# A graph and product-key memory block on one core: the dense head's passes divided 4 and 6 by slot instead of 5 and 5

## The reference, cut to what matters

```python
sim = einsum('pbnhd,pkhd->pbnhk', q, pk_keys)            # two sides, 128 keys each
scores, idx = top_k(sim, 16)                             # best 16 of each side
score = scores[0][..., :, None] + scores[1][..., None, :]
final_scores, pk_idx = top_k(score, 16)                  # best 16 of the pairs
final_scores = softmax(final_scores)
k = einsum('bnhk,bnhkd->bnhd', final_scores, keys_table[ind])    # 16 rows of 16384 per head
v = einsum('bnhk,bnhkd->bnhd', final_scores, values_table[ind])
attn = softmax(causal(einsum('bihd,bjhd->bhij', q_scaled, k)))   # then attn @ v @ Wo
```

## Time and profile before

| what | us |
|---|---|
| runs | 14943.0, 14952.5 (median), 15046.9 |
| profiled execution, its time | 14961.5 |
| its span, first to last instruction | 14959.7 |
| a batch, from its first L571 to the next batch's (14 batches) | 920.0 to 942.5 |

### The profile page before, as it was taken

How to read it: one execution, slowest core, us unless ns; L and a number is a source line. 1 busy time by engine, 2 the same in 40 slices (tenths; PEclk the granted TensorE clock), 3 DMA queues, 4 the chain that set the end, 5 groups by cost and what they waited for, 6 DMA issues and landing times.

```text
span 14959.7 us, 181203 instructions
## 1 busy us (share of the span) xinstructions
PE 8819.9 (59%) x51232; PEld 6784.1 (45%) x51232; DVE 7189.0 (48%) x32006; ACT 4890.6 (33%) x14163; POOL 6799.1 (45%) x7177
## 2 busy tenths in 40 slices
PE   4665655555565565556556555655555555556566
PEld 3444444444444444444444444444444444444454
DVE  5454454544545445444454544445454454544543
ACT  2333333333333333333333333333333333333332
POOL 4444444444444444444444444444444444444444
PEclk7777777777777777777777777777777777777777
DMA  3333333333333333333333333333333333333332
GB/s 93 102 103 103 99 103 101 100 101 100 101 101 104 105 100 102 102 100 103 102 102 100 103 102 100 103 101 104 102 102 104 98 103 104 103 100 96 99 109 92
DMA packets 445985, 1516.88 MB, mean 101 GB/s; under 512 B 123760, under 2 KB 141552, under 8 KB 379248
## 3 DMA queue, kind: packets, MB, share of 16 engines
q0 software_dynamic: 344064, 939.98, 21.3%
q1 hardware_dynamic: 100848, 564.37, 10.9%
HBM read 1499.66 MB, written 4.19 MB: 101 GB/s over the span
## 4 chain that ended last, share of the span: by engine, by line
PE 35%; another core or an unknown queue 27%; DVE 15%; issue 15%; ACT 7%; DVEq 0%; ACTq 0%; DMA 0%; SPq 0%
PE dense_ps L461 13%; PE comb_ps L571 6%; DVE wide L1106 5%; PE wideT_ps L447 5%; ACT expo L697 3%; PE score_ps L498 2%; PE front_ps L401 2%; PE probT_ps L504 2%; PE score_ps L437 2%; DVE onehot L990 1%; DVE onehot L997 1%; DVE hits L1070 1%; ACT wideT L632 1%; ACT prob L737 1%
## 5 line engine op out<-in xcount | busy, mean ns | idle before, releaser
L334 POOL DMA_INDIRECT got<-in_table,rows x7168 | 6797.2, 948 | 8123.9 <-PE comb_ps L571 5913.5
L1106 DVE SCALAR_TENSOR_TENSOR wide<-const_ps,rank,expo 128x128 f32<-128x128 f32 x8192 | 2303.7, 343 | 5572.5 <-remote 4357.0
L461 PE MATMUL dense_ps<-tab,wideT 128*128 128x256 f32 x16384 | 4435.4, 419 | 105.3 <-ACT kv_d L632 53.7
L447 PE MATMUL wideT_ps<-ident,wide 128*128 128x128 f32 x8192 | 1474.6, 311 | 4746.9 <-ACT wideT L632 2784.1
L461 PEld LDWEIGHTS dense_ps<-tab,wideT 128*128 128x128 f32 x16384 | 3338.7, 213 | 845.1 <-issue 309.7
L447 PEld LDWEIGHTS wideT_ps<-ident,wide 128*128 128x128 f32 x8192 | 1134.4, 160 | 5157.4 <-issue 4830.7
L632 ACT ACTIVATE wideT<-wideT_ps 128x512 f32<-128x512 f32 x2048 | 1217.8, 595 | 4674.7 <-remote 3415.3
L697 ACT ACTIVATE expo<-sim_d,shift 128x128 f32<-128x128 f32 x8192 | 2595.1, 393 | 0.6 <-DVEq L1051 0.2
L571 PE MATMUL comb_ps<-got,spread 128*32 128x256 f32 x14336 | 1021.1, 433 | 2.2 <-issue 2.2
L632 ACT ACTIVATE probT<-probT_ps 128x128 f32<-128x128 f32 (+3 forms) x512 | 223.6, 437 | 1556.0 <-remote 1250.7
L571 PEld LDWEIGHTS comb_ps<-got,spread 128*32 128x32 f32 x14336 | 463.8, 123 | 457.1 <-issue 257.5
(11 more groups left out here) (156 smaller groups left out, 8286.8 us busy)
## 6 DMA issues: line engine op xcount, KB each, us to landing
tab<-in_dense SPq DMA_DIRECT2D x512, 1024.0 KB
got<-in_table,rows POOLq DMA_INDIRECT x7168
adj_i<-in_adj SPq DMA_DIRECT2D x16, 1024.0 KB, 7.3
x_in<-in_x SPq DMA_DIRECT2D x16, 256.0 KB
out<-fin SPq DMA_DIRECT2D x16, 256.0 KB, 5.4
tab<-in_wqpk_t SPq DMA_DIRECT2D x1, 512.0 KB, 10.5
tab<-in_keys_t SPq DMA_DIRECT2D x1, 512.0 KB, 15.4
wq_sb<-in_wq SPq DMA_DIRECT2D x1, 512.0 KB, 14.2
```

The lines of the kernel that those rows point to most:

```text
L334: pool.indirect_dma_start(out=got[t % 2][:, g, :], out_offset=None, in_=table, in_offset=bass.IndirectOffsetOnAxis(ap=rows[buf(h)][:, t * ...
L447: mm = pe.transpose(wideT_ps[:, q * P:(q + 1) * P], wide[k % 2][:, q, :], ident[:, :])
L461: mm = pe.matmul(dense_ps[:, v * 2 * D:(v + 1) * 2 * D], wideT[k % 2][:, (2 * u + v) * P:(2 * u + v + 1) * P], tab[(k // CHUNK) % 2][:, (2 ...
L1106: last = dve.scalar_tensor_tensor(wide[k % 2][:, 2 * u + v, :], count_ps[:, v, :], rank1[:, 2 * half + v, key:key + 1], expo[k % 2][:, 2 * ...
```

## The change

The tuples of the middle batches are chosen by slot. The four slots with two passes stay. Every other odd slot (t = 1 or 3) gets `FOUR`, without the pass at w[4], and every other even slot (t = 0 or 2) gets `SIX`, with a second pass at w[0].

```diff
 ONE = (1, 1, 1, 1, 1)
 SIX = (2, 1, 1, 1, 1)
+FOUR = (1, 1, 1, 1, 0)
 FEW = (1, 1, 0, 0, 0)
 NONE = (0, 0, 0, 0, 0)
-MIDDLE = [ONE] + [FEW] * 2 + [ONE] * 12 + [FEW] * 2 + [ONE] * 11
+MIDDLE = [FEW if n in (1, 2, 15, 16) else FOUR if n % 2 else SIX for n in range(SLOTS)]
 ENDING = [SIX] + [FEW] * 2 + [SIX] * 12 + [FEW] * 2 + [SIX] * 2 + [ONE] * 6 + [NONE] * 3
```

## The result

The kernel after takes 15404.3 us (median of 3 runs, 15399.1 to 15409.6), against 14952.5: a ratio of 1.029, interval 1.024 to 1.034. It is slower by 452 us, or 30 us in each of the 15 batches. The forecast was 15095 with a range up to 15310: the sign was right, the size was a third of what came.

What follows compares the result with a forecast made beforehand. The prediction took a gather burst plus serial tail per slot as the bound. Its terms, 19.9 - 20.4 + 13.2 - 3.3 = +9.4 us a batch, +141 us over 15 batches, gave a median of 15095 us, range 14840 to 15310.

Steps and rivals of the forecast that it cites:

- What bounds the kernel: Each slot: about 3 us, a 20 us gather burst stalling TensorE's signals, 3 us more, then a serial tail.
- The sixth pass of the even slots: Second pass at w[0]: +2.96 us per t = 0 slot, +0.35 per t = 2 slot, +19.9 us a batch.
- The fifth pass of the odd slots: Dropping w[4] from the tail starts the move 1.7 us earlier per slot, -20.4 us a batch.
- the give-back: Combining products of ten odd slots after `SIX` fall from 2.26 to 1.93 us, -3.3 us a batch.
- The clock: Odd-slot tails without their multiply partly stay at half clock, slowing later TensorE products: +13.2 us a batch.
- the cold rival: Front and combining products run wholly at half clock: clock term 24 us a batch, 15255 us; chance 0.27.
- What costs nothing: ScalarE and VectorE instructions, SyncE's chunk loads and GpSimd's gather issue were taken to add no time.
- Warm: Rival: shorter tails still bring the clock back, so the clock term goes: 14895 us; chance 0.20.
- Faster: Rival: VectorE's chain slips under the burst, odd tails shorten 2.63 us a slot, clock holds: 14725 us; chance 0.13.

Runs made afterwards that it cites:

- reversed: Kernel before, given four passes (0, 1, 1, 1, 1) in even slots and six in odd ones: 15643.7 us, 1.040, first kind of chip.
- The fill: Kernel after plus four unread products in each four-pass tail: 15215.9 us, 1.011 on the first kind of chip; 9789.0 us, 1.021 on the second.
- slot0_five: Kernel after with five passes in slots 0 and 3: 15291.1 us, 1.024 against the kernel before, first kind of chip.
- the halves: Kernel after with the change kept only in t=0/t=1 slots, or only in t=2/t=3: 9734.8 and 9739.0 us, 1.016 each, second kind of chip.

## Why the prediction was wrong, step by step
**What bounds the kernel** held on the first kind of chip. Slots are a burst and a serial tail, the loss shows as GpSimd's wait for the combining products, and most of it was made in the tail. It does not hold on the second kind, of which the trace of before gave no sign.

**The sixth pass of the even slots: right at t = 0, wrong at t = 2.** Slots 0, 4, 8 and 12 now take 1802.90 / 56 = 32.19 us in batches 1 to 14; batch 15 had said 32.82. Slots 6, 10 and 18 take 1463.98 / 42 = 34.86, where it had said 33.07. "The t = 2 slots had mostly spent that already" was the step that failed: a sixth pass costs 0.9 to 1.15 us there with a warm tail ahead, not 0.35, and 2.5 with a cold one. Three slots of batch 15 stood for 84 in other surroundings. The traces show how they differ, if the stop is taken as the longest idle stretch of TensorE in a slot. In batch 15 these three slots get five multiplies done ahead of the stop, which begins 16.9 us into the slot on average, and one is left for the tail. In batches 1 to 14 TensorE gets about four done ahead of it with either tuple. The sixth pass therefore falls into the tail: the t = 2 slots have 1.1 multiplies there before and 2.0 after, and their tail grows from 7.3 to 11.4 us; the t = 0 slots go from 0.8 to 1.8 and from 7.2 to 10.8 us, while the stop gets shorter. Why batch 15 fits one more in is not shown. Together the two kinds cost 29.9 us a batch; less the 6.7 that belong to the clock it is 23.2, inside the bounds of 13 and 27.

**The fifth pass of the odd slots: overrated, then lost.** L438 starts 1.66 us earlier in t = 1 slots (32.99 to 31.33 us into the slot), which looks like the 1.7 forecast. But 0.38 of it is the faster L572 at the start of the slot, which the prediction counts by itself as the give-back, so the pass was worth 1.3 us. In t = 3 slots L438 starts 1.2 us earlier (31.68 to 30.49), and 1.1 is the pass. That is 14.4 us a batch for the 20.4 forecast, just inside its bounds. The middle between two kinds of slot was the error: in 114 of the 168 odd slots of the kernel before L437 starts within 0.4 us of the end of the lift, where VectorE decides and the prediction itself had 1.2. In t = 3 slots the part from L438 to the next slot became 1.6 us longer, of which 0.54 lies in L438 and 1.05 in L402 over all six slots, so nothing is left: +0.4 us a slot. The comparison I drew on, 0.86 us for a sixth pass in odd slots, was of no use: in `reversed` it cost 4.6.

**The clock: the right mechanism, under-priced, on the first kind of chip.** From the rows of the kernel after: L438 in t = 1, 6 x 0.50; L438 and L402 in t = 3, 6 x 1.62; L572 at t = 2, 6 x 1.12 (with slot 27 taken like the other five of t = 3). That is 3.0 + 9.7 + 6.7 = 19.4 us a batch, against 13.2 forecast and 24 for the cold rival. With L438 and L402 taken whole in all six t = 3 slots it is 19.3. "Denser than the tails of slots 1 and 15, so I give it part of the price" was the error: most tails with no multiply were as cold as those. After slots 9, 13, 17 and 21 L572 took over 3.1 us in every batch; after slots 5 and 25 it was 2.9 on average, and slot 23 kept part of its clock too (L402 2.72 us). The give-back after `SIX` came as forecast: L572 takes 1.93 us in all ten odd slots. The fill, which takes time of its own, gives back 12.6 to 18 us a batch (medians as they are, or 1.8 points of 15036 us), so the size is confirmed only roughly. The Trainium skill, "TensorE: Matmul & The Clock Gate", section "HAM oscillation — how this bites in real kernels", was on the cold side, and the trace mostly bore it out: 3.64 against 1.93 us for the products behind a gapped tail, in 68 of 84 cases at half clock for most of them. The second kind of chip goes further that way: there the tails with a multiply fall to half clock too.

**What costs nothing: not so.** The four slots with two passes were put at 0 and cost 5.1 us a batch, nearly all in slot 1, and `slot0_five` shows that slot 0's sixth pass is the cause. I had priced a pass in the slot it stands in and never asked the slot after it.

**The sum of the misses**, forecast to measured: t = 0 -2.8, t = 1 +1.7, t = 2 +9.1, t = 3 +7.8, the four +5.1, together 20.9, which is 30.3 - 9.4. By the terms of the prediction it is: sixth pass 23.2 for 19.9, fifth pass -14.4 for -20.4, clock 19.4 for 13.2, and 5.1 for the 0 of the four slots; the give-back of 3.3 held in its ten slots. These make 30.0 of the 30.3. Each miss has the same sign, and the fifth pass and the clock weigh most. Of the rivals the cold one was nearest, 15255, and 149 us short: its clock term of 24 was nearer than mine though too large, and the other three misses were not in it. Warm (14895) falls with L438. Faster (14725) asked for a tail 2.5 us shorter, and the t = 1 slots got 1.2 shorter.

**Still open:** whether it is the gather burst that holds TensorE's signals back on the first kind (the run with half the gathers never met such a chip), how slot 0 reaches slot 1, why batch 15 fits one more pass in ahead of the stop, and why the t = 3 slots of the second kind gain less in the whole than in the halves.

## What to carry to other kernels
When work is taken out of a latency-bound stretch of TensorE, ask first whether it was what brought the clock back: its removal can cost more in the products behind it than it saved, and a few unread products in its place are a quick test, if the kernel before gets them too. A price from another part of the same trace holds only if the neighbours are the same too; compare the slot after as well as the slot itself. The cost of one pass more and the gain of one pass less are different numbers here (+2.5 and -1.2 us), so moving work between two slots can lose in both directions.

## What was not expected of the hardware
The same kernel takes 14930 to 15040 us on some chips and 9580 to 9590 on others, 1.56 times as fast, with the same instructions. On the first, TensorE goes idle for some 13 us in each slot while GpSimd's gathers are issued, and by the trace's semaphore events the signal behind a turn arrives a median 13 to 14 us late when it is given 6 to 8 us into a burst. The later it is given, the shorter the delay: signals given from 8 to 22 us into a burst of 16 gathers all arrive 22.6 to 22.7 us (medians) after its start, some 3 us after its last gather, in the kernel before and in the kernel after. That ties the stop to the burst in time, though not yet as its cause. On the second kind the median delay is 0.01 us at every distance from the burst's start. It is not the speed of the transfers: the packets of 4096 bytes take a median 159 ns on both. Ratios also change between the kinds (1.029 and 1.038 for the change, 1.011 and 1.021 with the fill), so a ratio is carried only within one. What makes the chips differ isn't shown by any run here.
